# Feed-forward rows of all token tiles get places of their own, and the steps over the slots stand in a new order

## The reference

```python
xn = _layernorm(x)
# attention: 16 heads of 16 channels
u, v, q, k = split(silu(layer_norm(xn) @ W1 + b1), 4)
scores = einsum('bqhd,bkhd->bhqk', qh, kh)
av = einsum('bhqk,bkhd->bqhd', silu(scores) / S, vh)
y = layer_norm(av * u, gamma, beta) @ W2 + b2
# feed-forward, with weights rounded to -1, 0, 1 times one scale
h = layer_norm(xn, ln1_g, ln1_b) @ ternary(w1).T + b1      # 256 -> 1024
h = layer_norm(gelu(h), ln2_g, ln2_b)
out = x + y + h @ ternary(w2).T + b2                       # 1024 -> 256
```

## Time and profile before

| | us |
|---|---|
| runs | 1597.40, 1601.91, 1602.28 (median 1601.91) |
| the profiled execution's own time | 1597.45 |
| span of its instructions | 1595.7 |
| PE busy | 1482.5 (93%) |
| ACT busy | 1223.6 (77%) |
| DVE busy | 896.9 (56%) |
| POOL busy | 98.7 (6%) |
| mean granted clock of PE | 0.986 |

### The profile page before, as it was taken

The page is one execution under the profiler, slowest core; times in us unless marked ns, Lnnn a source line. Parts: engine busy times, 40 slices in busy tenths (PEclk is TensorE's granted clock), DMA queues, the critical chain, the costliest instruction groups (busy, mean ns, idle before and its releaser), DMA issues.

```text
span 1595.7 us, 27804 instructions
## 1 busy us (share of the span) xinstructions
PE 1482.5 (93%) x9826; PEld 778.7 (49%) x9826; DVE 896.9 (56%) x1716; ACT 1223.6 (77%) x1285; POOL 98.7 (6%) x193
## 2 busy tenths in 40 slices
PE   4799999999999999999999999999999999999986
PEld 3345455454554454544545455545455445554443
DVE  4466734666366653666546674376734666457543
ACT  2578886888868887788877888678886888868883
POOL 2000100001000100001000010000100010000000
PEclk9799999999999999999999999999999999999998
DMA  6561034510444106421165113451044410543100
GB/s 182 112 132 35 20 85 107 127 54 1 108 118 94 54 14 139 113 54 54 41 134 125 38 37 80 107 132 54 1 96 111 113 54 1 127 110 82 27 1 27
DMA packets 62330, 123.68 MB, mean 78 GB/s; under 512 B 7664, under 2 KB 9328, under 8 KB 61168
## 3 DMA queue, kind: packets, MB, share of 16 engines
q1 hardware_dynamic: 62192, 121.81, 32.4%
HBM read 79.84 MB, written 41.94 MB: 76 GB/s over the span
## 4 chain that ended last, share of the span: by engine, by line
issue 93%; POOLq 6%; POOL 1%; DVE 0%; DVEq 0%
POOLq L517 3%; POOLq L509 1%; POOLq L493 1%; POOL rs L503 1%; POOLq L502 0%; POOLq L511 0%; POOLq L507 0%; POOLq L505 0%; POOLq L519 0%; POOLq L522 0%; POOLq L203 0%; POOL rs L494 0%; DVE part L764 0%; DVEq L203 0%; POOLq L536 0%
## 5 line engine op out<-in xcount | busy, mean ns | idle before, releaser
L550 ACT ACTIVATE attn<-scores 128x1024 f32<-128x1024 f32 x1024 | 983.2, 1025 | 260.6 <-PE scores L920 259.7
L939 PE MATMUL outs<-attn,V 128*32 128x512 f32 x4096 | 501.0, 607 | 0.0
L920 PE MATMUL scores<-QS,KS 64*128 64x512 f32 x2048 | 407.9, 461 | 74.8 <-ACT attn L550 51.9
L920 PEld LDWEIGHTS scores<-QS,KS 64*128 64x128 f32 x2048 | 165.3, 186 | 390.6 <-ACT attn L550 314.6
L939 PEld LDWEIGHTS outs<-attn,V 128*32 128x32 f32 x4096 | 108.0, 110 | 240.8 <-issue 240.7
L793 DVE SCALAR_TENSOR_TENSOR hid<-fill,ratq,fb1b 128x512 f32<-128x512 f32 x128 | 96.2, 751 | 75.3 <-PE fill L994 70.0
L810 DVE TENSOR_TENSOR tmp<-fill,l2g 128x512 f32<-128x512 f32 x128 | 88.5, 692 | 88.8 <-PE fill L1003 77.5
L1010 PE MATMUL fill<-Wq,hgh 128*128 128x256 f32 x512 | 130.6, 293 | 0.0
L976 PE MATMUL fill<-xp,W1h 128*128 128x512 f32 x384 | 125.5, 408 | 2.3 <-DVE xp L834 1.5
L1010 PE MATMUL fill<-Wq,hgl 128*128 128x256 f32 x512 | 124.9, 282 | 0.0
L1010 PEld LDWEIGHTS fill<-Wq,hgh 128*128 128x128 f32 x512 | 97.3, 190 | 18.0 <-issue 10.4
(11 more groups left out here) (110 smaller groups left out, 1415.1 us busy)
## 6 DMA issues: line engine op xcount, KB each, us to landing
QS<-q_scratch SPq DMA_DIRECT2D x128, 256.0 KB, 7.2
k_scratch<-kst SPq DMA_DIRECT2D x64, 256.0 KB
q_scratch<-qst SPq DMA_DIRECT2D x64, 256.0 KB
KS<-k_scratch SPq DMA_DIRECT2D x64, 256.0 KB, 4.1
KS<-k_scratch SPq DMA_DIRECT2D x128, 128.0 KB, 5.0
xin<-in_x SPq DMA_DIRECT2D x8, 1024.0 KB, 6.2
out_dram<-part SPq DMA_DIRECT2D x16, 512.0 KB, 2.6
w1raw<-in_W SPq DMA_DIRECT2D x1, 1024.0 KB, 7.0
```

Source lines behind the costliest of these rows:

```text
L550: nc.scalar.activation(attn_of(g)[:, 2 * hf:2 * hf + 2, :], SP[:, 2 * hf:2 * hf + 2, :], ACT.Silu).then_inc(s_silu, 1)
L920: ins = mm(SP[:, j, :], KS[rows, pair, t * P:(t + 1) * P], QS[rows, pair - c * PPC, h * HALF:(h + 1) * HALF], start=True, stop=True)
L939: ins = mm(OP[32 * j:32 * j + 32, g // RUN % 2, :], V[:, t, c * HPC // 2 + j, o * DH:o * DH + 2 * DH], attn_of(g)[:, n, :], start=(o == 0 ...
```

## The change

The hidden rows get eight places instead of four: tiles 0 to 3 stay over xp, tiles 4 and 5 lie over `vraw` (the V products), and tiles 6 and 7 get 8 KB a partition of space that was free. `f1.4.0` on DVE now waits until vs.1 has read vraw. xt.i comes after g of tile i alone. The order of the steps over the slots is new throughout; the 96 steps are the same, and each does what it did. The rows of the table, two a line (pair n in line n), a slash between the two slots:

The rest of the diff:

```diff
-for _i in range(NP - 2):
-    in_order(f"g.{2 * _i + 1}.1", f"f1.{2 * _i + 4}.0")
-in_order("g.5.1", "xt.0")
-in_order("g.7.1", "xt.2")
+for _i in range(NP):
+    in_order(f"g.{_i}.1", f"xt.{_i}")
+in_order("vs.1", "f1.4.0")
+in_order("g.5.1", "v.0")
...
+        vraw_at = top[0]
         vraw = sb("vraw", [P, T, D], F32)
+        hid45 = at("hid45", [P, 2, HID], F32, vraw_at)
+        hid67 = sb("hid67", [P, 2, HID], F32)
         xh_at = top[0]
...
-        hid = at("hid", [P, 4, HID], F32, xh_at)
+        hid03 = at("hid03", [P, 4, HID], F32, xh_at)
...
+        def hid_pair(i):
+
+            return hid03[:, 2 * i:2 * i + 2, :] if i < NP // 2 else (hid45, hid67)[i - NP // 2][:, :, :]
+
         def hid_of(t):
 
-            return hid[:, t % 4, :]
+            return hid_pair(t // 2)[:, t % 2, :]
...
-                    rows = hid[:, 2 * i % 4:2 * i % 4 + 2, :]
+                    rows = hid_pair(i)
...
                     t, hf = a
+                    if me == ("f1", T // 2, 0):
+
+                        dve.wait_ge(s_v, 2 * b + 2)
                     wait_filled(dve, b, me)
```

More of the change, by code:

```diff
@@ L60 @@
 TABLE = (
-    "zt.0 zs.0 zt.1",
-    "zs.1",
-    "a.0 zs.2 zt.2",
-    "",
-    "",
-    "a.1 a.2 zs.3 zt.3",
-    "a.3 u.1.0",
-    "",
-    "k.1.0 px q.1.0",
-    "u.0.0 u.1.1",
-    "",
[L72 to L78, removed]
+    "zs.0 zt.0 zt.1",
+    "",
+    "zt.2 zs.1",
+    "a.0 vs.1 zt.3",
+    "",
+    "a.1 zs.2",
+    "zs.3 a.2",
+    "",
+    "a.3 k.1.0",
+    "u.0.1 q.1.0 px k.1.1",
+    "q.1.1 u.1.0 y.1 y.0",
+    "u.0.0",
+    "u.1.1 f1.0.0",
+    "",
+    "",
+    "y.2 f1.0.1 f1.1.0 f1.1.1 f1.2.0 f1.2.1 y.3 gelu.0",
+    "",
+    "f1.3.0 ln2.0 nrm2.0",
+    "",
     "f1.3.1",
-    "",
     "g.0.0 g.0.1",
     "",
[L83 to L86, removed]
+    "f1.4.0 f2.0 g.1.0 g.1.1",
+    "gelu.1 f1.4.1 ln2.1",
+    "f2.1",
     "",
@@ L89 @@
     "",
[L90 to L94, removed]
-    "",
-    "ln1 f1.6.1",
-    "",
-    "",
-    "xn.0",
-    "nrm2.2 g.4.0 g.4.1",
-    "",
[L102 to L105, removed]
-    "",
-    "xn.2 g.6.0",
-    "g.6.1",
+    "f2.2",
+    "",
+    "g.3.0 g.3.1",
+    "",
+    "f1.5.0",
+    "f1.5.1 f1.6.0 f1.6.1 gelu.2 ln2.2 f2.3",
+    "nrm2.2 f1.7.0",
+    "ln1",
+    "f1.7.1",
+    "g.4.0",
+    "xn.0 g.4.1",
+    "xt.0",
+    "",
+    "gelu.3 xn.1 f2.4 g.5.0 g.5.1 v.0",
+    "xt.1",
+    "ln2.3 f2.5 nrm2.3",
+    "k.0.0",
+    "",
+    "",
+    "g.6.0 g.6.1",
+    "q.0.0",
+    "",
+    "xn.2 v.1 xt.2 xn.3",
+    "",
     "",
     "f2.6",
-    "k.0.0 g.7.0",
     "",
[L113 to L118, removed]
+    "v.2 xt.3",
+    "k.0.1",
+    "g.7.0",
+    "",
+    "g.7.1 q.0.1",
     "",
     "v.3",
-    "k.0.1 q.0.1",
     "",
-    "f2.7",
-    "vs.0",
+    "f2.7 vs.0",
 )
```

## The result

| | us |
|---|---|
| changed kernel, median | 1637.37 (1636.15 to 1640.17) |
| kernel before, median beside it | 1599.69 (1597.40 to 1602.28) |
| ratio | 1.0232, 95% interval 1.0205 to 1.0258 |
| span of the profiled execution | 1635.7, before 1595.7 |
| mean granted clock of PE | 0.971, before 0.986 |

Each kernel has four runs here; the 1601.91 that stands ahead is the median of three. The forecast was 1616 with a range of 1587 to 1640: the direction and the range held, and the rise of 38 us is more than twice the 14 to 16 that I had worked out.

The account below looks back on a forecast made before the run. PE was asked for 175.1 us of a body's 190.30, with light and gelu pairs bound by ACT. Order (+4) and slow clock (+12) on the profiled 1597.45 gave 1613.5, stated as 1616, range 1587 to 1640.

Parts of the forecast that it names:

- pairs 7 to 15: Same PE steps, but f1.4.1 moves into the gelu.1 pair: 52.0 us, before 53.05, so -1.0 a body.
- Pair 4: k.1.1 waits for k.1.0's write to land, 7.41 us after k.1.0 started on ACT; PE idles 2.5; pair lasts 13.9.
- 2.6 us worked out from the Trainium skill: Rule for landing of k.1.0's 256 KB write; would make the stall 0.9 us instead of 3.15, time about 1583.
- The slow clock: PE drops to clock 0.50 behind pair 4's hole: 1.5 us a body, +12 in all.
- pairs 5 and 6: Pair 5 at 7.65 us without the wait for q, pair 6 at 5.7; +18 over all bodies with slow clock.
- Rival 1: The stall in pair 4 comes without the slow clock: +4, 1604 us; chance 0.14.
- Rivals 2 to 4: In order: k write lands early, 1584 (0.12); packing worth more, 1590 to 1597 (0.08); second stall, pair 19, 1630 (0.16).
- pair 19: Counted at 5.5 us with xt.0's copy on ACT last; the rival had xt.0 stall 2 us in seven bodies, 0.16.
- Pairs 21 to 31 ... 58.7: 2.03 us of steps leave, but k.0.0 and q.0.0 stand alone: 58.7 us, before 59.93, so -1.2 a body.
- 9 us for that in bodies 1 and 7: q.0.1 a pair earlier ends the scores' wait for KS and the slow PE after it: -9 in all.
- pairs 0 to 3: Three a and four zt instead of four a, four zt and one u: 20.7 us, before 24.0.
- body 0 apart: Body 0 has no a steps to hide in: +2.

Follow-up runs that it names:

- e5_places: The kernel before with the eight places, the new wait of f1.4.0 and vs.1 moved up to pair 1; 1599.52 us, ratio 1.0007.
- e1_k_apart: The changed kernel with k.1.1 and u.1.0 exchanged, so that k.1.1 comes a pair later than k.1.0; 1614.72 us, ratio 1.0105.
- e8_y_first: The changed kernel with k.1.1 a pair later and y.1 and y.0 ahead of k.1.1 and q.1.1; 1592.94 us, ratio 0.9946.
- e2_hold: The changed kernel with five of six last KS loads and the last QS loads held until the next batch's first scores; 1626.44 us, ratio 1.0180.
- e12_hold_q: The changed kernel with only the last QS loads held back, from the second on; the six KS loads stay in pair 31; 1634.70 us, ratio 1.0224.
- e6_pe_out: The changed kernel with PE's loop over batches written out, the other four engines' loops kept; 1638.85 us, ratio 1.0234.
- e7_all_out: The changed kernel with the loops of all five engines written out; 1607.59 us, ratio 1.0042.
- e4_before_early: The kernel before with the slot of k.0.1 and q.0.1 two slots (a pair) earlier; 1609.17 us, ratio 1.0061.
- e9_before_out: The kernel before with the loops of all five engines written out; 1602.61 us, ratio 1.0019.

## Why the prediction was right in kind and wrong in size

- *The bound.* PE's 3.18 us for the attention work and the prices by columns hold: the forecast of pairs 7 to 15 was 52.0 (measured 52.3), of 16 to 20 33.0 (33.4), of 21 to 30 51.5 (50.9). The places cost nothing (e5_places).
- *Pair 4.* 13.9 forecast, 13.82 measured, with the wait, its releaser and the hole behind it as worked out. e1_k_apart and e8_y_first take it away. The 2.6 us worked out from the Trainium skill ("DMA: Bandwidth & Descriptors", section "Anatomy of one DMA — SWDGE (gpsimd) path") do not hold for this write: ACT waited until 7.45 us after the first evacuation, 5.5 after the split. That section is on DMAs issued from GpSimd, and SP issues every DMA here, so the runs say nothing against it where it is meant.
- *The slow clock.* It came in all eight bodies behind the 2.5 us hole, and pairs 5 and 6 became 20.7 us longer where 18 was forecast. Rival 1 falls, and with it the other ways in which the wait would have been cheap.
- *Rivals 2 to 4.* No early landing, and no extra packing (7 to 20 cost a little more than forecast). Nor did pair 19 stall: 4.9, less than the 5.5 allowed.
- *The step that failed* is the term "Pairs 21 to 31 ... 58.7" (batch 3: 60.81 measured), in which I carried pair 31 over from before as it was. In its steps it is as it was; but q.0.1 came a pair earlier, and in the very sentence in which I booked 9 us for that in bodies 1 and 7 I did not follow SP's loads forward to where they now fall. They fall on the turn of the loops. Pair 31 and the end cost 15.0 us where the sum had nothing: 13.2 in the five turns, and the rest mostly at the end of the program. Behind the turn stands a slow stretch all five times, where the kernel before has one three times; in bodies 2 to 6 pairs 0 to 3 won 13.4 us where the forecast had 16.5, though with all loops written out they are at 19.97, below the 20.7 forecast. That is about half of why they won 29 in all and not 35; the other half is body 0, which won 0.4 instead of 3.3 and for which the row "body 0 apart" had 2. e2_hold shows the loads to be the cause of the longer part (21.2 to 12.1 us), e12_hold_q that it is not the QS loads it holds, and e6_pe_out, e7_all_out and batch 6, which leaves the loop without a jump, that the hole as such belongs to the turn.
- *The remainder.* Of 25 us that the forecast of the sum lacked, 15 are pair 31 and the end, 6 pairs 0 to 3, 3 pairs 16 to 20, 3 pairs 5 and 6, and the rest are parts of 2 us and less that nearly cancel. In the last body pairs 21 to 30 take 3.1 us more than before, with two slow stretches in them. They don't belong to the order: the same steps take 48.43 us in e1_k_apart, which has no slow stretch there, 50.05 in e8_y_first with one, and 51.52 in the changed kernel with two.
- What stays open: whether the wait at the turn is the fetch of instructions. The runs show that it belongs to the jump back (it goes with the loop of the engine that has it), that no semaphore ends it, and that loads issued just ahead of it lengthen it; what the engine does in it no row shows.

## What to carry to other kernels

When a step moves, follow what it issues on every queue to the place where it now lands, and look at what else stands there, a loop's end included; a gain booked at one end of a shifted transfer has a price at the other. A single buffer that is written out by a DMA sets a least distance between its two users: evacuation, split and landing (1.9 + 5.5 us here) have to fit between them. And an idle hole on TensorE costs more than its length, as the work behind it may run at half the clock.

## What the runs showed of the hardware that was not expected

- The jump back of a loop costs PE 1.7 to 2.2 us in the kernel before, whose loads come after it, and 3.9 to 4.5 in the new orders, with ten loads issued in the 6 us from 2.7 us ahead of the hole on. DVE is 4.1 to 6.5 us late at its own jump, most of it hidden until PE's is gone (e6_pe_out), and stops once more behind it (5.39 us between two instructions in e4_before_early).
- A hole of 1.86 us on PE was followed by the lower clock at the turn from batch 3 to 4 of the kernel before, and not at the turn from batch 2 to 3, where it was 1.86 us too and the 16 matmuls of attn times V took 1.93 and not 3.20; holes of 2.51 to 2.57 were followed by it eight times out of eight.
- Writing five loops out won 1.9% in the new order (ratios 1.0232 and 1.0042) and none in the old as it stood (e9_before_out), where a late transfer took the place of the turn; with that transfer a pair earlier it won 2.1% (1.0061 and 0.9855).
- Two writes of 256 KB issued one behind the other take 5.5 us from the end of the split to the release of ACT (7.45 - 1.91 in the changed kernel, 5.50 in the earlier trace rows), more than twice the 2.6 us from issue to landing of a store of 512 KB.
